# Recurrence of a graph network on one Trainium2 core: the adjacency product in quarter tiles, and an earlier high part of r*h

## The reference

```python
h = relu(layernorm(x))
for _ in range(3):
    a_in = einsum('nm,bmd->bnd', adj, h)       # a_out is the same: both matrices are adj
    av = concatenate([a_in, a_in], -1)
    z = sigmoid(lin(av, w3) + lin(h, u3))
    r = sigmoid(lin(av, w4) + lin(h, u3))
    hv = tanh(lin(av, w5) + lin(r * h, u5))
    h = (1 - z) * h + z * hv
x = x + h
```

## Time and profile before

| | us |
|---|---|
| median of 3 runs | 1593.96 |
| lowest, highest | 1591.88, 1594.06 |
| the profiled execution's own time | 1595.16 |
| its span, first to last instruction | 1593.1 |
| PE busy | 1510.5 (95%) |
| DVE busy | 1243.9 (78%) |
| ACT busy | 993.0 (62%) |
| POOL busy | 533.7 (34%) |

### The profile page before, as it was taken

The page is one execution under the profiler, slowest core; times in us unless marked ns, Lnnn a source line. Parts: engine busy times, 40 slices in busy tenths (PEclk is TensorE's granted clock), DMA queues, the critical chain, the costliest instruction groups (busy, mean ns, idle before and its releaser), DMA issues.

```text
span 1593.1 us, 40455 instructions
## 1 busy us (share of the span) xinstructions
PE 1510.5 (95%) x16248; PEld 1299.4 (82%) x16248; DVE 1243.9 (78%) x2511; ACT 993.0 (62%) x1793; POOL 533.7 (34%) x622
## 2 busy tenths in 40 slices
PE   3899999899999987799999999999999999999997
PEld 3789989798888876588888888888888888888885
DVE  2787887988899986677877877877777777778666
ACT  3676677667777774565666566655665566566553
POOL 1666766667787893300101111111111111111000
PEclk9999999999999998899999999999999999999998
DMA  9200000003322242100000000000000000000000
GB/s 251 82 3 0 0 0 1 15 16 61 61 53 53 56 78 29 27 0 1 27 1 1 27 0 0 26 0 0 26 0 0 26 0 0 27 1 0 27 1 26
DMA packets 36760, 40.12 MB, mean 25 GB/s; under 512 B 11840, under 2 KB 31808, under 8 KB 36672
## 3 DMA queue, kind: packets, MB, share of 16 engines
q0 software_dynamic: 4608, 16.78, 5.6%
q1 hardware_dynamic: 32064, 22.10, 4.8%
HBM read 13.71 MB, written 8.39 MB: 14 GB/s over the span
## 4 chain that ended last, share of the span: by engine, by line
PE 68%; DVE 15%; ACT 7%; issue 5%; POOL 4%; DMA 1%; SPq 0%; DVEq 0%; POOLq 0%; ACTq 0%
PE ring L99 30%; PE scores L99 23%; PE scores L1545 3%; PE ring L1343 2%; PE scores L1307 2%; DVE rhp_lo L1196 2%; PE ring L1490 2%; DVE total L955 2%; POOL s L530 1%; PE ring L1380 1%; ACT rhp_hi L824 1%; ACT later_w L814 1%; PE ring L1508 1%; PE ring L1463 1%; ACT later_w L808 1%
## 5 line engine op out<-in xcount | busy, mean ns | idle before, releaser
L1196 DVE TENSOR_TENSOR rhp_lo<-r,rhp_hi 128x1024 fp32r<-128x1024 f32 x48 | 58.8, 1225 | 157.0 <-ACT rhp_hi L824 157.0
L530 POOL TENSOR_TENSOR s<-s,mx 128x512 f32<-128x512 f32 x128 | 137.9, 1102 | 46.3 <-DVE mx L951 46.3
L536 POOL TENSOR_TENSOR s<-s,rtotal 128x512 f32<-128x512 f32 x128 | 131.4, 1056 | 36.7 <-DVE rtotal L957 36.5
L594 POOL TENSOR_TENSOR r_var_eps<-r_mean_var,eps 128x4 f32<-128x4 f32 x16 | 8.1, 509 | 384.3 <-DVE r_mean_var L1105 384.3
L669 ACT ACTIVATE s<-s 128x512 f32<-128x512 f32 x128 | 78.4, 644 | 76.1 <-POOL s L530 75.9
L839 ACT ACTIVATE hv<-scores,bias 128x512 f32<-128x512 f32 x96 | 66.1, 689 | 83.6 <-PE scores L99 83.6
L946 DVE SCALAR_TENSOR_TENSOR s<-scores,mask 128x512 f32<-128x512 f32 x128 | 87.2, 681 | 32.4 <-PE scores L1307 32.4
L808 ACT ACTIVATE later_w<-ring 128x512 f32<-128x512 f32 x64 | 34.8, 595 | 121.9 <-PE ring L1508 121.9
L681 ACT ACTIVATE pT<-ring 128x512 f32<-128x512 f32 x128 | 66.1, 604 | 47.1 <-PE ring L1343 47.1
L951 DVE TENSOR_REDUCE mx<-s 128x8 f32<-128x512 f32 x128 | 87.9, 686 | 4.4
L857 ACT ACTIVATE r<-r,bias_half 128x512 f32<-128x512 f32 x96 | 64.3, 717 | 37.7 <-DVE r L1221 37.7
(11 more groups left out here) (295 smaller groups left out, 5251.2 us busy)
## 6 DMA issues: line engine op xcount, KB each, us to landing
x<-beta_less_one POOLq DMA_DIRECT2D x16, 512.0 KB, 4.6
x<-o POOLq DMA_DIRECT2D x16, 512.0 KB, 6.5
out_x<-x SPq DMA_DIRECT2D x16, 512.0 KB, 2.9
x<-in_x SPq DMA_DIRECT2D x1, 6656.0 KB, 30.5
later_w<-in_L_gnn_w_w SPq DMA_DIRECT2D x3, 512.0 KB, 7.2
x<-in_x SPq DMA_DIRECT2D x1, 1024.0 KB, 10.9
stage<-in_L_gnn_w_qkv SPq DMA_DIRECT2D x3, 256.0 KB, 3.0
x<-in_x SPq DMA_DIRECT2D x1, 512.0 KB, 3.5
```

The costliest lines, as they stand in the source:

```text
L530: pool.tensor_tensor(sr, sr, mx[:, r, :].unsqueeze(2).to_broadcast([P, CT * 2, N]), ALU.subtract).then_inc(s_shifted, 1)
L536: pool.tensor_tensor(sr, sr, rtotal[:, r, :].unsqueeze(2).to_broadcast([P, CT * 2, N]), ALU.mult).then_inc(p_ready, 1)
L1196: dve.tensor_tensor(rhp.lo[:], r[:], f32(rhp.hi[:]), ALU.subtract).then_inc(rh_lo_ready, 1)
```

## The change

The adjacency product is cut along the diagonal of `adjT`. In place of one 128x128 by 128x128 matmul it issues four 64x64 by 64x64 ones: the graph `g` of the tile gives the 64 rows that are contracted, `c` gives 64 of the 128 features. The products with the zero blocks are gone. The four address different quarters of the PE array. A half now has 32 float32 matmuls, which is 64 instructions with 64 columns each in place of 16 with 128. The result of graph g goes to bank g (not bank m), in the order m, t, q; the high and low part of the aggregate are taken bank by bank, with a strided write that puts them where they lay before. Both banks' signals come with the last four matmuls (t = 3, m = 1), where m = 0 was signalled halfway before.

ACT takes the high part of r*h behind the tok copies and ahead of the tanh of z; before, it came behind that tanh and behind the copy of u3's product for m = 0. Two waits of PE ahead of the adjacency product are made with `wait_apart`.

```diff
                     if not s.first:
+                        act.wait_ge(rh_done, n)
+                        if isinstance(n, int) and n == 1:
+                            act.wait_ge(x_plus_o, 16 * CHUNKS)
+                            act.wait_ge(x_plus_beta, 16 * CHUNKS)
+                        act.activation(rhp.hi[:], r[:], ACT.Copy).then_inc(rh_hi_ready, 1)
+                    if not s.first:
                         for m in range(FT):
                             act.wait_ge(z_added, (n - 1) * FT + m + 1)
                             act.activation(z[:, m, :], z[:, m, :], ACT.Tanh, bias=bias_half[:, 0, m:m + 1], scale=0.5)\
...
                     if not s.last:
                         act.wait_ge(hu_ready, n * FT + 1)
                         act.activation(hu[:, 0, :], ring[:, 2, :], ACT.Copy).then_inc(hu_copied, 1)
-                    if not s.first:
-                        act.wait_ge(rh_done, n)
...
-                        act.activation(rhp.hi[:], r[:], ACT.Copy).then_inc(rh_hi_ready, 1)
...
-                        for m in range(FT):
-                            act.wait_ge(agg_ready, n * FT + m + 1)
-                            act.activation(agg.hi[:, m, :], high[:, m, :], ACT.Copy).then_inc(agg_hi_ready, 1)
+                        for g in range(2):
+                            act.wait_ge(agg_ready, n * FT + g + 1)
+                            act.activation(agg.hi[:].rearrange("p m (t g q) -> p g m t q", t=CT, g=2)[:, g],
+                                           high[:, g, :].rearrange("p (m t q) -> p m t q", m=FT, t=CT), ACT.Copy)\
+                                .then_inc(agg_hi_ready, 1)
...
-                        for m in range(FT):
-                            dve.wait_ge(agg_hi_ready, n * FT + m + 1)
-                            dve.tensor_tensor(agg.lo[:, m, :], high[:, m, :], f32(agg.hi[:, m, :]),
+                        for g in range(2):
+                            dve.wait_ge(agg_hi_ready, n * FT + g + 1)
+                            dve.tensor_tensor(agg.lo[:].rearrange("p m (t g q) -> p g m t q", t=CT, g=2)[:, g],
+                                              high[:, g, :].rearrange("p (m t q) -> p m t q", m=FT, t=CT),
+                                              f32(agg.hi[:]).rearrange("p m (t g q) -> p g m t q", t=CT, g=2)[:, g],
                                               ALU.subtract).then_inc(agg_lo_ready, 1)
...
-                            pe.wait_ge(tok_copied, (s.later - 1) * 2)
+                            wait_apart(pe, tok_copied, (s.later - 1) * 2)
...
-                            pe.wait_ge(z_added, n * FT)
+                            wait_apart(pe, z_added, n * FT)
...
-                        for m in range(FT):
-                            for t in range(CT):
-                                last = pe.matmul(high[:, m, t * P:(t + 1) * P], rows[:, t, m * P:(m + 1) * P],
-                                                 adjT[:], start=True, stop=True)
-                            last.then_inc(agg_ready, 1)
+                        for t in range(CT):
+                            for m in range(FT):
+                                for g in range(2):
+                                    own = slice(g * N, (g + 1) * N)
+                                    for c in range(2):
+                                        f = m * P + c * N
+                                        last = pe.matmul(
+                                            high[c * N:(c + 1) * N, g, (m * CT + t) * N:(m * CT + t + 1) * N],
+                                            rows[own, t, f:f + N], adjT[own, own], start=True, stop=True)
+                                    if t == CT - 1 and m == FT - 1:
+                                        last.then_inc(agg_ready, 1)
```

More of the change, by code:

```diff
@@ L818, in half @@
                         act.activation(hu[:, 0, :], ring[:, 2, :], ACT.Copy).then_inc(hu_copied, 1)
-                    if not s.first:
-                        act.wait_ge(rh_done, n)
-                        if isinstance(n, int) and n == 1:
-                            act.wait_ge(x_plus_o, 16 * CHUNKS)
-                            act.wait_ge(x_plus_beta, 16 * CHUNKS)
-                        act.activation(rhp.hi[:], r[:], ACT.Copy).then_inc(rh_hi_ready, 1)
                     if s.graph_b is not None:
```

## The result

The changed kernel takes 1572.4 us (median of 4 runs, 1572.3 to 1575.3) against 1593.95 us before. The ratio is 0.9872, with a 95% interval of 0.9855 to 0.9889. It is 21.5 us faster, where 28.5 us were forecast. The profiled execution took 1572.46 us.

The account below looks back on a forecast made before the run. PE was taken to bound most recurrence halves, DVE k = 0 and 5. Gains of 9.0, 13.2, 3.7, 1.05, 1.0 and 0.6 made 28.5 us, so 1565.5 us; band 1561 to 1570 (chance 0.62), range 1557 to 1584.

Parts of the forecast that it names:

- Three kinds of halves: Recurrence halves: k = 1, 3 PE-bound without wait; k = 2, 4 and last four PE-bound with one; k = 0, 5 through DVE.
- k = 0 and 5: Halves whose chain goes through DVE, in groups with graph attention: gain only 0.17 and 0.15 us, most handed back.
- The product's own length: Adjacency product's path in one half: 1.95 us before, 1.35 us after, so PE saves 0.60 us in each half it bounds.
- b: Time from first to last start of the adjacency product's 64 small matmuls in one half, taken as 0.88 us.
- Entry 0.32 and exit 0.15 us: Cost of stepping from u3's matmul into the small tiles, and from their last start back to full-size work.
- A: Rival: instruction supply paces the adjacency product's quarters, b = 1.07 to 1.38; gain 19 to 4 us, 1575 to 1589; chance 0.22.
- C: Rival: two quarters sharing 64 array rows don't work at the same time, b = 1.76, time 1608; chance 0.05.
- The order on ACT: Earlier high part of r*h removes u5's 0.34 us wait for its low part in k = 2 and 4.
- Rival D: The move on ACT gives nothing because another wait stands in its place: 6 us less, time 1572; chance 0.05.
- one cut of 1.87 us: Instruction issue cut a run of small tiles; zero taken for the recurrence, two such cuts (4 us) put into the range.
- the prediction's own formula: Whole kernel: gain = 28.5 - 48 x (b - 0.88); below 0.88 only the 33 PE-bound halves gain.
- rival B: Adjacency product faster than a quarter's own pace, b = 0.66: gain about 36 us, time 1557; chance 0.06.

## Why the prediction was right, and where its sizes were off

**Three kinds of halves.** Right. The PE-bound halves gained alike, those with the wait gained the wait on top, and k = 0 and 5 gave most of it back; moving 1.73 us of DVE's work out of their way brought it again.

**The product's own length.** The mechanism held (16 rounds for each quarter, no sharing between quarters), the term was small by a little: b = 0.94 us and not 0.88. The pace is 0.0586 us and not 0.056, and the first round takes longer: the second starts 0.107 us behind it. The estimate was 16 x 0.056 = 0.90 us, of which 0.88 was taken. Entry 0.32 and exit 0.15 us came as computed. 0.06 us in each of 47 halves is about 3 us of the difference. The supply of instructions (A) did not bind, and neither did shared rows (C).

**The order on ACT.** Right in detail. DVE in half k = 2 of the changed kernel, which answers the earlier trace rows:

```profile
1036.23 1.23 DVE L1198 TENSOR_TENSOR rhp_lo<-r,rhp_hi 128x1024 fp32r<-128x1024 f32 x1 [1.93 <-ACT rhp_hi L816]
1038.24 0.42 DVE L1138 TENSOR_REDUCE g_total<-e 128x4 f32<-128x256 f32 x1 [0.79 <-ACT e L786]
...
1039.79 1.29 DVE L1206 TENSOR_TENSOR agg_lo<-scores,agg_hi 128x512 fp32r<-128x512 f32 x2
```

The low part of r*h ends at 1037.46, 0.9 us ahead of u5's start at 1038.34, and its wait is gone. Attention's sums now wait for the exponential, as forecast. The aggregate's low part ends at 1041.08 and w4 starts at 1041.60, with 0.5 us to spare (forecast 0.4). The order alone was worth 0.35 us a half.

**The sum of terms.** The total for k = 2 and 4 was right to 0.08 us, but writing it as 0.60 for the product and 0.34 for the order misattributes it. The tiles alone gave 0 there. A reader who took the terms one by one would have expected some 15 us of the tiles alone and found 4.3. Rival D has the same mistake in its price: with the wait left standing, 18 halves would have lost their whole gain of about 0.94 us, some 17 us and not 6.

**k = 0 and 5.** Forecast 0.15 and 0.17, got 0.09 in straight code. The difference is mostly b again (0.06 us): here it counts in full, because the signal for the aggregate comes at the run's end.

**The step that failed: instructions.** The prediction saw one cut of 1.87 us in an attention layer and took zero for the recurrence, with two cuts in the range. What happened was of another kind: the loop grew by 48 loads and 48 matmuls a half, 576 instructions in six halves, and each of its four passes back now waits 0.4 to 1.0 us, 2.2 us more in sum than before where 0.7 us less was counted. That is another 3 us. The question "what does PE still have when it jumps back" was not asked; the page's count of instruction packets could have raised it.

**On the other side** the first half took 24.98 us instead of 26.48, 1.2 us better than counted, and that is luck. PE waits 8.9 us for ACT behind the product there, so its length hardly shows: the two tiles of 64 rows and 128 columns, whose product is 0.8 us longer, took 25.01 us. The half runs partly at the lower granted clock (0.79 in the mean, 0.81 before), and where that falls differs from run to run: the kernel before without its loop runs the same code there as the kernel before and took 25.28 us, at 0.85. So at least 1.2 of the 23.8 us that the recurrence gained can't be credited to the shorter product. The stretch ahead of it took 1.1 us more in this profile, and the medians differ by 21.5 us. No run tells why that stretch varies.

**The chances.** The measured time lies in the gap between the forecast's band (to 1570) and rival A's (from 1575). It is also, to 0.4 us, the time that rival D stands for (1572). That is a coincidence: D says that another wait takes the place of the one for the low part of r*h, and the traces show that wait gone from all 18 halves. By the prediction's own formula b = 0.94 gives 1568 us; 3 of the other 4 us are the loop's way back. Of the signs that it named, a group's period fell by 2.9 us in straight code, not 3.4, for the same reason as b; PE's idle time ahead of the leaving transposes came as said, and w4's product never waits for the aggregate's low part. Two small slips in the bands: with only 33 halves gaining below b = 0.88, b = 0.8 gives 1563 us and not 1561, and rival B's 0.66 gives 1558 us. Faster was clear.

## What to carry to other kernels

A product that is shortened on the bounding engine gains only where its successor's other input is already early, so make that input early first, and expect the two edits to be worth more together than apart. After such a change look for the hole it leaves: work of the same engine that waits behind the new bound may fit in it (here 1.73 us of statistics in a hole of 1.56 to 2.65 us, worth some 13 us). Small tiles multiply instructions; count those in a hardware loop, and look at the first instruction behind the jump and at the instruction packets while the loop runs.

## What the runs showed of the hardware that was not expected

- Four 64x64 tiles of the PE array work side by side: 64 float32 instructions of 64 columns in 0.94 us, in either order of the tiles. Two tiles of 64 rows and 128 columns take 1.73 us for 32 instructions, no faster for each tile than the full array's 0.112 us: cutting only the rows brought nothing here, while the weights stayed 128 columns wide.
- Going into small tiles costs 0.32 us behind a 512-column matmul (0.23 us without the change of tile), and coming back 0.15 us from last to first start (0.03 us).
- A loop with 1816 loads and matmuls of PE in each pass waits 0.4 to 1.0 us on each way back, and instruction packets come all through it; with 1432 or 1240 it doesn't wait, and none come. Where between 1432 and 1816 the limit lies, and why the wait varies from pass to pass, stays open.
- Strided writes in runs of 64 elements cost neither ACT (1.10 us for two against 1.18) nor DVE (1.29 against 1.29) anything.
